# The work between two cross-attention layers moves pair by pair into the second attention's loop

## Chip, cores and metric

One core of one Trainium2 chip runs the program. The metric is device time in microseconds from launch to end; the median of three runs of the kernel before is given with the profile. TensorE (PE) multiplies matrices, VectorE (DVE), ScalarE (ACT) and GpSimd (POOL) do the elementwise work, and SyncE (SP) issues the DMAs. PE writes only to the eight PSUM banks, and POOL can't read them.

## The reference

Two layers over a batch of 16, with 56 queries of 128 numbers each and a context of 1500 rows of 96. Cut to what is computed:

```python
# layer 0 (16 heads of 8)
q, k, v = jnp.split(x @ w_qkv + b_qkv, 3, axis=-1)
x = layer_norm(x + mha(q, k, v) @ w_so + b_so, ln_g, ln_b)
ca = mha(x @ w_q + b_q, y @ w_k + b_k, y @ w_v + b_v) @ w_co + b_co   # y: context
x = layer_norm(x + ca, ln_g, ln_b)
h = relu(x @ w1 + b1)              # 128 -> 512
h = relu(h @ w2 + b2)              # 512 -> 512
x = layer_norm(x + h @ w3 + b3, ln_g, ln_b)
# layer 1 (16 heads of 64)
h = layer_norm(x, gamma, beta)
Q, K, V = h @ Wq, y @ Wk, y @ Wv   # split in heads
attn = softmax(Q K^T) / 8
x = x + (attn V) @ Wo + bo
```

## The kernel before

All 16 batches' queries are handled as 896 tokens, or as eight tiles of two batches (a pair, 112 tokens). The program is a row of blocks; at the end of each, all engines meet, and within one each engine works down its own queue in the order written, with semaphores between them.

1. Opening block and self-attention (to 69 us).
2. Block A (69 to 95 us, lines 687 to 747): projection, norm, and the first cross-attention's queries. PE makes the queries once as 128 rows (`a_all`, L704) and then once more for each of four groups of heads, three times replicated to 96 rows (`wq3`, L713). ACT writes the fp16 part of each (L744), DVE the rest below it (L727), into `Q16`. Between these stand three transposes of a context.
3. The first cross-attention's loop over batches (95 to 470 us). POOL lays the queries of the next batch out by head (`Qst`, L773, and `Qmx`, L350).
4. The block between the layers (470 to 579 us, lines 1044 to 1192). For all eight tiles at once: output projection, norm (mean and variance on DVE, root on ACT, reciprocal on DVE), the three products of the feed-forward network in fp32 over 448 columns at a time (L1088, L1096, L1103), two more norms, and, since each head's key product can be taken into the queries (`Wqk` = Wq Wk^T per head), 32 fp32 products that give every batch's queries in context space (L1127). ACT writes their fp16 part (L1161), DVE the rest (L1189), to the tensor `QK` for all batches. Beside them the weights are turned (L1076) and multiplied (L1109, L1116). The last 12 of these 32 products have the score pieces of batch 0 between them.
5. The second cross-attention's loop (579 to 1104 us): one pass per batch, `body(i, par)` with batch b = 2i + par, of 14 steps c on each engine. In step c (under 12) PE makes the transposed scores of 125 keys in two halves, of three fp16 products each (L1283 to L1285, three PSUM banks), ACT takes their exponential (L1376), and POOL, or DVE in each third step, splits off the low part (`Pl`, L1266 and L1465). From step 2 on PE multiplies chunk c - 2 with the context (L1301 to L1303, 63 products a step).

Beside that the softmax maximum of the next batch is found: 21 score pieces of 500 keys (`score_piece1`, L1005), two or three a step from step 1, in two banks in turn. DVE reduces each (`reduce_piece1`, L1014), and PE waits for it as the first line says:

```python
wait_for(pe, n_red, n * 21 + max(k - 1, 0))   # piece k needs k - 1 reductions
...
if has_b and c < NC:
    scores_t(i, par, c, 0)
for k in pieces[:1]:
    score_piece1(pe, i, par, k)
if has_b and c < NC:
    scores_t(i, par, c, 1)
```

The first piece of a step thus stands between the two halves of the scores. At step 10 DVE takes the maximum over the pieces (`negate_maximum`, L1439 to L1447), at step 12 PE turns it (L1333) and DVE lays it beside the queries (`lay_maximum`, L1452), for which the next batch's scores wait (`n_mlaid`). At the start of a batch DVE first divides the batch before by its sums (`finish_batch`, L1405 and L1409), at steps 4 to 7 PE, ACT and DVE turn that output in the bank W1, and in even batches PE projects a pair at step 8 (L1322) and DVE adds residual and bias at step 9 (L1423, L1427). SP loads the halves of the next batch's context and queries (`load_halves`, L994 and L997) as soon as the slot is free.

## Time and profile before

| | us |
|---|---|
| median of three runs | 1106.84 (1106.81 to 1107.83) |
| the profiled execution, its own time | 1106.37 |
| its span, first to last instruction | 1104.60 |
| before the first cross-attention (0 to 95.4) | 95.4 |
| first cross-attention (95.4 to 470.15) | 374.75 |
| between the layers (470.15 to 578.80) | 108.65 |
| second cross-attention (578.80 to 1104.60) | 525.80 |

The profile is of one execution; its instruction times are compared with its own time. Busy time is the sum of an engine's instructions; PE's are pipelined, and their ends modelled. A group is named by line, engine, operation and out<-in tiles. "[idle before <-releaser]" behind an instruction is the engine's idle time and who ended it. PEclk is the granted share of 2.4 GHz.

### The profile page before, as it was taken

To read this page: it belongs to the slowest core of one execution; us is meant where nothing else is said; L and a number is where in the kernel's file an instruction comes from. 1 tells how busy PE (TensorE), PEld (TensorE's weight loads), DVE (VectorE), ACT (ScalarE), POOL (GpSimd) and SP (SyncE) were. 2 spreads that over 40 slices of the span, in tenths; PEclk is the share of its full clock that TensorE was granted. 3 is DMA by queue.
4 is the path that set the end of the run, shared out by engine and by line. 5 is a ranking of instruction groups with operands and counts; after the bars stand their busy time and mean duration, and the time that the engine had idled before them with its cause. 6 is when DMAs were issued, how large, how long until landed. Compare 5 with 4: busy or idle time off the path is not lost. (4 is left out here: it accounts for less than half of the span.)

```text
span 1104.6 us, 31648 instructions
## 1 busy us (share of the span) xinstructions
PE 1026.3 (93%) x12060; PEld 742.5 (67%) x12060; DVE 748.1 (68%) x1409; ACT 571.4 (52%) x1139; POOL 389.8 (35%) x273
## 2 busy tenths in 40 slices
PE   5977899999999999979688999999999999999997
PEld 2552577777777776646325777777777778777786
DVE  4657788887888778321794776777676767767752
ACT  2533577777777776631444544445444444544442
POOL 4821121111211123030105554545455454646542
PEclk9988899999999999989798999999999999999998
DMA  3501544444444443030002111111111111012100
GB/s 105 144 2 70 145 133 135 126 152 140 128 132 139 141 123 91 2 99 1 0 23 76 56 56 38 55 38 39 54 56 54 41 49 51 28 52 56 35 4 4
DMA packets 48461, 79.41 MB, mean 72 GB/s; under 512 B 8802, under 2 KB 35252, under 8 KB 48404
## 3 DMA queue, kind: packets, MB, share of 16 engines
q1 hardware_dynamic: 48404, 78.61, 23.8%
q8 instruction: 40, 0.66, 0.3%
q14 instruction: 17, 0.14, 0.0%
HBM read 51.13 MB, written 21.96 MB: 66 GB/s over the span
## 5 line engine op out<-in xcount | busy, mean ns | idle before, releaser
L1376 ACT ACTIVATE P<-PS 125x448 f32<-125x448 f32 x384 | 207.1, 544 | 270.3 <-PE PS L1285 268.4
L1266 POOL TENSOR_TENSOR Pl<-P 125x896 f16<-125x896 f32 x128 | 229.9, 1801 | 242.3 <-ACT P L1376 242.3
L1014 DVE TENSOR_REDUCE m<-PS 128x1 f32<-128x500 f32 x336 | 220.8, 675 | 120.1 <-PE PS L1005 118.3
L920 DVE TENSOR_REDUCE m_part<-PS 128x1 f32<-128x500 f32 x336 | 210.5, 673 | 54.8 <-PE PS L822 53.3
L1301 PE MATMUL PS<-cNh,P 125*128 125x97 f16 x1344 | 198.0, 208 | 0.1
L1303 PE MATMUL PS<-cNh,Pl 125*128 125x97 f16 x1344 | 197.4, 207 | 0.0
L1302 PE MATMUL PS<-cNl,P 125*128 125x96 f16 x1344 | 196.8, 206 | 0.0
L898 ACT ACTIVATE Pb<-PS 125x448 f32<-125x448 f32 x384 | 186.0, 547 | 19.5 <-PE PS L797 18.5
L1302 PEld LDWEIGHTS PS<-cNl,P 125*128 125x128 bf16 x1344 | 131.9, 98 | 25.5 <-issue 0.2
L1301 PEld LDWEIGHTS PS<-cNh,P 125*128 125x128 bf16 x1344 | 131.2, 98 | 15.8 <-issue 3.2
L1283 PE MATMUL PS<-Qh,cTh 110*125 110x448 f16 x384 | 139.0, 362 | 1.3 <-DVE Qh L1452 1.3
L822 PE MATMUL PS<-KH,Qmx 128*128 128x500 f16 x336 | 129.2, 387 | 8.5 <-DVE m_part L920 4.1
L1284 PE MATMUL PS<-Ql,cTh 96*125 96x448 f16 x384 | 136.8, 356 | 0.0
L773 POOL TENSOR_TENSOR Qst<-Q,tab 96x224 f16<-96x224 f32 (+1 forms) x64 | 33.7, 556 | 289.6 <-DVE Qst L960 281.2
L1285 PE MATMUL PS<-Qh,cTl 96*125 96x448 f16 x384 | 135.6, 353 | 0.0
L1303 PEld LDWEIGHTS PS<-cNh,Pl 125*128 125x128 f16 x1344 | 131.1, 98 | 0.0
L1005 PE MATMUL PS<-cTh,Qh 96*128 96x500 f16 x336 | 119.3, 377 | 6.6 <-DMA Qh<-QK 3.5
L797 PE MATMUL PS<-Qst,Kst 110*125 110x224 f16 x768 | 110.8, 263 | 4.9 <-DMA Kst<-k_halves 2.1
L797 PEld LDWEIGHTS PS<-Qst,Kst 110*125 110x125 f16 x768 | 87.8, 136 | 30.4 <-ACT Pb L898 7.7
L808 PE MATMUL PS<-Pb,Vst 125*32 125x112 f32 x3072 | 93.3, 262 | 0.0
L1465 DVE TENSOR_TENSOR Pl<-P 125x896 f16<-125x896 f32 x64 | 70.3, 1099 | 28.3 <-ACT P L1376 28.2
L808 PEld LDWEIGHTS PS<-Pb,Vst 125*32 125x32 f32 x3072 | 70.4, 109 | 19.6 <-issue 15.4
(170 smaller groups left out, 1530.0 us busy)
## 6 DMA issues: line engine op xcount, KB each, us to landing
Kst<-k_halves SPq DMA_DIRECT2D x144, 125.0 KB, 2.8
k_halves<-KH SPq DMA_DIRECT2D x16, 750.0 KB, 3.2
cx<-in_ctx SPq DMA_DIRECT2D x16, 562.5 KB
d_cx<-in_ctx SPq DMA_DIRECT2D x16, 562.5 KB
c_halves<-cHi SPq DMA_DIRECT2D x16, 281.2 KB, 2.6
c_halves<-cLo SPq DMA_DIRECT2D x16, 281.2 KB, 3.0
cTh<-c_halves SPq DMA_DIRECT2D x16, 281.2 KB, 3.0
cTl<-c_halves SPq DMA_DIRECT2D x16, 281.2 KB, 3.8
```

What stands on the lines that cost most here:

```text
L797: mm = pe.matmul(PS[0:KC, u % 3, (g % 2) * 224:(g % 2 + 1) * 224], Kst[:, par, g, c * KC:(c + 1) * KC], Qst[:, par, g, :], start=True, sto ...
L808: mm = pe.matmul(PS[32 * (p % 4):32 * (p % 4) + 32, OB, (p // 4) * TP:(p // 4 + 1) * TP], Vst[:, par, c, p, :], Pb[:, c % NPB, p * TP:(p + ...
L898: nc.scalar.activation(Pb[:, c % NPB, half * HALF:(half + 1) * HALF], PS[0:KC, u % 3, 0:HALF], ACT.Exp, scale=SCALE0).then_inc(exp_done, 1)
L920: nc.vector.tensor_reduce(m_part[:, t, part:part + 1], PS[:, 6 + k % 2, 0:SP], AX.X, ALU.max).then_inc(s_reduced, 1)
L1014: nc.vector.tensor_reduce(m21[:, t, part:part + 1], PS[:, S1[k % 2], 0:SP], AX.X, ALU.max).then_inc(n_red, 1)
L1266: nc.gpsimd.tensor_tensor(Pl[:, c % NP], P1[:, c % NP], high, ALU.subtract).then_inc(n_low_p, 1)
L1283: pe.matmul(o, cTh[:, par, at], Qh[:, par, cols], start=True, stop=False)
L1284: pe.matmul(o, cTh[0:DC, par, at], Ql[:, par, cols], start=False, stop=False)
L1301: pe.matmul(o, high, cNh[:, par, c, :], start=(c == 0 and t % 4 == 0), stop=False, skip_group_check=True)
L1302: pe.matmul(o[:, 0:DC], high, cNl[:, par, c, :], start=False, stop=False, skip_group_check=True)
L1303: mm = pe.matmul(o, Pl[:, c % NP, cols], cNh[:, par, c, :], start=False, stop=(c == NC - 1), skip_group_check=True)
L1376: nc.scalar.activation(P1[:, c % NP, half * HALF:(half + 1) * HALF], PS[0:KC, u % 3, 0:HALF], ACT.Exp).then_inc(n_exp, 1)
```

## The change

- **Block A.** The four replicated products are gone, with `wq3` and `bq3`. ACT writes the fp16 part of the 128-row queries (`Qall`), DVE its rest (`Qrest`), and SP copies both group by group with twelve DMAs into `Q16`. POOL waits for them before the first `Qst`.
- **First attention.** POOL splits w1, w2 and w3, times 64, into two fp16 halves in batch 0 (`split_weights`).
- **Between the layers.** Only pair 0 goes all the way there, and pair 1 up to the second hidden layer. All feed-forward and query products use three fp16 products (high x high, high x low, low x high) in place of one fp32. The root of the variance is taken on DVE, by a guess from the bits and three Newton steps (`spread_of`), in place of ACT's root. `QK` for all batches becomes `QKs` for one pair. The halves and queries of batches 0 and 1 are both loaded here.
- **Second attention.** An odd batch 2i + 1 does the first part for pair i + 2 (`pair_ahead`): projection, `norm_cross`, hidden layers, and at its last step `hidden_3`. The even batch 2i + 2 does the second part for that pair (`pair_behind`, there i + 1): `norm_twice`, `turn_pair`, and in steps 3, 5, 7 and 10 `absorb`, which makes four heads' queries for both batches. All use the bank W1 in turn with the output's turning and projection, hence the added waits.

The diff, cut. Left out are declarations, the small helpers `out_project`, `turn_pair` (one PE operation each), `keep_pair` and `keep_hidden` (two and four ACT operations of 112 columns), `residual`, `take_attention`, `move_residual` (two, one and one POOL operations on 112 x 128), `hidden_3` (12 products as in `hidden_2`) and `queries_high` (one ACT copy of 448 columns), the removed lines of the block between, and its new PE, ACT and POOL queues, which have the same calls in the order of DVE's.

```diff
+                sp.wait_ge(a_high, 1)
+                for block_row in range(2):
+                    for g in range(G):
+                        sp.dma_start(Q16[32 * block_row:32 * block_row + 32, g, :], Qall[32 * g:32 * g + 32, :]).then_inc(q_in, 16)
+                sp.wait_ge(a_low, 1)
+                for g in range(G):
+                    sp.dma_start(Q16[64:96, g, :], Qrest[32 * g:32 * g + 32, :]).then_inc(q_in, 16)
...
+                    for n, (weight, halves) in enumerate(((w1s, w1x), (w2s, w2x), (w3s, w3x))):
+                        nc.gpsimd.tensor_scalar(weight[:], weight[:], WS, None, ALU.mult).then_inc(w_scaled, 1)
+                        pool.wait_ge(w_scaled, n + 1)
+                        nc.gpsimd.tensor_copy(halves[:, 0], weight[:]).then_inc(w_high, 1)
+                        pool.wait_ge(w_high, n + 1)
+                        nc.gpsimd.tensor_tensor(halves[:, 1], weight[:], halves[:, 0], ALU.subtract).then_inc(w_split, 1)
+                    nc.gpsimd.tensor_tensor(rows[:, R_B3, :], rows[:, R_B3, :], rows[:, R_B, :], ALU.add).then_inc(rows_added, 1)
...
-        def load_halves(sp, i, par, half, queries_made=None):
+        def load_halves(sp, i, par, half, ahead=False):
             slot, n = (par + 1) % 2, i * 2 + par + 1
             keys, queries = ((cTh, Qh), (cTl, Ql))[half]
-            if half == 0:
+            if half == 0 and not ahead:
                 wait_for(sp, n_st, (n - 1) * 2 * NC)
             at = bass.ds(n, 1)
             sp.dma_start(keys[0:DC, slot:slot + 1, :], c_halves[at, half].rearrange("b p k -> p b k")).then_inc(n_in[half][slot], 16)
-            if queries_made is not None:
-                sp.wait_ge(queries_made, H)
-            sp.dma_start(queries[0:DC, slot].rearrange("p (h q) -> p h q", h=H).unsqueeze(1), QK[:, half, at]).then_inc(n_in[half][slot], 16)
+            sp.wait_ge((g_high, g_low)[half], (i + (par + 1) // 2) * 4 + 4)
+            sp.dma_start(queries[0:DC, slot], QKs[:, half, slot].rearrange("p h q -> p (h q)")).then_inc(n_in[half][slot], 16)
...
+        def spread_of(dve, link, at, k, src):
+            dve.wait_ge(link, at)
+            nc.vector.bn_stats(st6[:, k], src).then_inc(link, 1)
+            dve.wait_ge(link, at + 1)
+            nc.vector.memset(passed[:], 0.0)
+            nc.vector.bn_aggr(mv[:, k], st6[:, k]).then_inc(link, 1)
+            dve.wait_ge(link, at + 2)
+            nc.vector.tensor_scalar(half_var[:, k:k + 1], mv[:, k, 1:2], EPS, -0.5, ALU.add, ALU.mult).then_inc(link, 1)
+            dve.wait_ge(link, at + 3)
+            nc.vector.tensor_scalar(root[:, k:k + 1].bitcast(I32), half_var[:, k:k + 1].bitcast(I32), -0.5, ROOT_GUESS, ALU.mult, ALU.add).then_inc(link, 1)
+            for n in range(ROOT_STEPS):
+                dve.wait_ge(link, at + 4 + 2 * n)
+                nc.vector.tensor_scalar(grown[:, k:k + 1], root[:, k:k + 1], root[:, k:k + 1], half_var[:, k:k + 1], ALU.mult, ALU.mult).then_inc(link, 1)
+                dve.wait_ge(link, at + 5 + 2 * n)
+                nc.vector.tensor_scalar(root[:, k:k + 1], grown[:, k:k + 1], 1.5, root[:, k:k + 1], ALU.add, ALU.mult).then_inc(link, 1)
+            dve.wait_ge(link, at + SPREAD)
+        def norm_cross(dve, t, bank):
+            dve.wait_ge(f_proj, t + 1)
+            nc.vector.tensor_tensor(wk[:].unsqueeze(1), PS[0:TP, bank, 0:D].unsqueeze(1), X[:, bass.ds(t, 1), :], ALU.add).then_inc(f_link, 1)
+            spread_of(dve, f_link, t * LINKS_A + 1, 0, wk[:])
+            nc.vector.tensor_scalar(nm[:], wk[:], mv[:, 0, 0:1], root[:, 0:1], ALU.subtract, ALU.mult).then_inc(f_normed, 1)
+        def split_pair(dve, t, k):
+            dve.wait_ge((f_kept, e_kept)[k], t + 1)
+            nc.vector.tensor_tensor(T16[:, k, 1], T32[:, k], T16[:, k, 0], ALU.subtract).then_inc((f_split, e_split)[k], 1)
+        def hidden_1(pe, t, bank):
+            pe.wait_ge(f_split, t + 1)
+            for m in range(4):
+                for n, (w, v) in enumerate(TERMS):
+                    mm = pe.matmul(PS[:, bank, m * TP:(m + 1) * TP], w1x[:, w, m * 128:(m + 1) * 128], T16[:, 0, v], start=(n == 0), stop=(n == 2))
+            mm.then_inc(f1, 1)
+        def hidden_2(pe, t, m, bank):
+            if m == 0:
+                pe.wait_ge(f1_split, t + 1)
+            for k in range(4):
+                for n, (w, v) in enumerate(TERMS):
+                    mm = pe.matmul(PS[:, bank, m * TP:(m + 1) * TP], w2x[:, w, k, m * 128:(m + 1) * 128], hid16[:, 0, v, k],
+                                   start=(k == 0 and n == 0), stop=(k == 3 and n == 2))
+            if m == 3:
+                mm.then_inc(f2, 1)
+        def split_hidden(pool, t, k):
+            kept, high, split = ((f1_kept, f1_high, f1_split), (f2_kept, f2_high, f2_split))[k]
+            pool.wait_ge(kept, t + 1)
+            nc.gpsimd.tensor_tensor(hid16[:, k, 0].rearrange("p m c -> p (m c)"), hid[:, k].rearrange("p m c -> p (m c)"),
+                                    one[:].broadcast_to([128, 4 * TP]), ALU.mult).then_inc(high, 1)
+            pool.wait_ge(high, t + 1)
+            nc.gpsimd.tensor_tensor(hid16[:, k, 1], hid[:, k], hid16[:, k, 0], ALU.subtract).then_inc(split, 1)
+        def norm_twice(dve, t, bank):
+            dve.wait_ge(f3, t + 1)
+            dve.wait_ge(f_residual, t * 2 + 2)
+            nc.vector.scalar_tensor_tensor(out=wk2[:], in0=PS[0:TP, bank, 0:D], scalar=1 / WS, in1=Xm[:], op0=ALU.mult, op1=ALU.add).then_inc(e_link, 1)
+            at = t * LINKS_B + 1
+            spread_of(dve, e_link, at, 1, wk2[:])
+            nc.vector.scalar_tensor_tensor(out=wk2[:], in0=wk2[:], scalar=mv[:, 1, 0:1], in1=rows[:, R_G, :],
+                                           op0=ALU.subtract, op1=ALU.mult).then_inc(e_link, 1)
+            dve.wait_ge(e_link, at + SPREAD + 1)
+            wait_for(dve, x_moved, t)
+            nc.vector.scalar_tensor_tensor(out=Xn[:], in0=wk2[:], scalar=root[:, 1:2], in1=rows[:, R_B, :],
+                                           op0=ALU.mult, op1=ALU.add).then_inc(e_link, 1)
+            spread_of(dve, e_link, at + SPREAD + 2, 1, Xn[:])
+            nc.vector.tensor_scalar(nm2[:], Xn[:], mv[:, 1, 0:1], root[:, 1:2], ALU.subtract, ALU.mult).then_inc(e_normed, 1)
+        def absorb(pe, t, r, bank):
+            if r == 0:
+                pe.wait_ge(e_split, t + 1)
+            for k in range(4):
+                for n, (w, v) in enumerate(TERMS):
+                    mm = pe.matmul(PS[0:DC, bank, k * TP:(k + 1) * TP], Wqk[:, w, 4 * r + k, :], T16[:, 1, v], start=(n == 0), stop=(n == 2))
+            mm.then_inc(g_made, 1)
+        def queries_low(dve, t, r, bank):
+            dve.wait_ge(g_high, t * 4 + r + 1)
+            if r == 0:
+                wait_for(dve, n_in[1][1], t * 32)
+            for j in range(2):
+                low = nc.vector.scalar_tensor_tensor(out=QKs[:, 1, j, 4 * r:4 * r + 4, :],
+                                                     in0=PS[0:DC, bank, 0:4 * TP].rearrange("p (h j q) -> p j h q", h=4, j=2)[:, j],
+                                                     scalar=1 / WS, in1=QKs[:, 0, j, 4 * r:4 * r + 4, :], op0=ALU.mult, op1=ALU.subtract)
+            low.then_inc(g_low, 1)
...
+                norm_cross(dve, 0, 0)
+                split_pair(dve, 0, 0)
...
+                norm_twice(dve, 0, 1)
+                norm_cross(dve, 1, W1)
+                split_pair(dve, 0, 1)
+                for r in range(4):
+                    queries_low(dve, 0, r, 1 - r % 2)
+                split_pair(dve, 1, 0)
+                for k in range(NPC):
+                    reduce_piece1(dve, -1, 1, k)
+        weights.close()
...
+                        has_p, t = pair_behind(i, par)
+                        if has_p and c == 2:
+                            move_residual(pool, t)
+                        has_p, t = pair_ahead(i, par)
+                        if has_p and c == 2:
+                            residual(pool, t)
+                            if not isinstance(t, int) or t + 1 < NT:
+                                take_attention(pool, t + 1)
+                        if has_p and c == 5:
+                            split_hidden(pool, t, 0)
+                        if has_p and c == 11:
+                            split_hidden(pool, t, 1)
+                over_pairs(pool, body, before=((-1, 1),), last=3)
...
+                        has_p, t = pair_behind(i, par)
+                        if has_p and c == 2:
+                            turn_pair(pe, t, 1, W1)
+                        if has_p and c in R_STEP:
+                            if has_old and c in (5, 7):
+                                pe.wait_ge(n_ot, (b - 1) * 2 + (c - 3) // 2)
+                            if has_old and c == 10:
+                                pe.wait_ge(n_y, i)
+                            elif not has_old and c > 3:
+                                pe.wait_ge(g_low, t * 4 + R_STEP[c])
+                            absorb(pe, t, R_STEP[c], W1)
+                        if has_p and has_old and c in (4, 6, 8):
+                            pe.wait_ge(g_low, t * 4 + c // 2 - 1)
+                        if has_b and has_old and c == 4 and pair_ahead(i, par)[0]:
+                            pe.wait_ge(f1_kept, pair_ahead(i, par)[1] + 1)
                         if has_b and has_old and c in (4, 6):
                             turn_output(b - 1, (c - 4) // 2)
                         if has_b and has_old and par == 0 and c == 8:
                             project(i - 1)
+                        if has_p and c == NC:
+                            pe.wait_ge(g_low, t * 4 + 4)
+                        has_p, t = pair_ahead(i, par)
+                        if has_p:
+                            if c == 0:
+                                out_project(pe, t, W1)
+                            if c == 2:
+                                turn_pair(pe, t, 0, W1)
+                            if c == 3:
+                                hidden_1(pe, t, W1)
+                            if c == 7:
+                                pe.wait_ge(n_ot, (b - 1) * 2 + 2)
+                            if 7 <= c < 11:
+                                hidden_2(pe, t, c - 7, W1)
+                            if c == NC:
+                                pe.wait_ge(f2_kept, t + 1)
+                        if isinstance(i, int) and b == -1 and c == NC:
+                            pe.wait_ge(f2_kept, 2)
                         if has_1 and c == NC:
                             turn_maximum(i, par)
+                        if c == NC + 1 and par == 1 and (has_p or (isinstance(i, int) and i < 0)):
+                            pe.wait_ge(n_mlaid, b + 2)
+                            hidden_3(pe, t, W1)
...
+                        has_p, t = pair_behind(i, par)
+                        if has_p and c == 0:
+                            norm_twice(dve, t, W1)
+                        if has_p and c == 3:
+                            split_pair(dve, t, 1)
+                        if has_p and c - 1 in R_STEP:
+                            queries_low(dve, t, R_STEP[c - 1], W1)
+                        has_p, t = pair_ahead(i, par)
+                        if has_p and c == 1:
+                            norm_cross(dve, t, W1)
+                        if has_p and c == 3:
+                            split_pair(dve, t, 0)
```

## Rows read from the trace of the kernel before

**Rows 1.** Busy time by engine; granted clock in 40 slices of the span.

```profile
PE 1026.3 (93%) x12060; PEld 742.5 (67%) x12060; DVE 748.1 (68%) x1409; ACT 571.4 (52%) x1139; POOL 389.8 (35%) x273
...
PEclk9988899999999999989798999999999999999998
```

**Rows 2.** Busy time by stretch: from:to, length, engines (instructions), clock, DMA share, GB/s.

```profile
470.15:578.80 108.65, 86.74 (x349) 46.08 (x349) 55.22 (x145) 36.08 (x55) 12.66 (x6) 0.91 0.11 31
...
742.30:806.10 63.80, 63.69 (x757) 49.65 (x756) 45.37 (x81) 29.81 (x58) 33.34 (x19) 1.00 0.15 48
...
588.00:592.60 4.60, 4.55 (x12) 2.50 (x13) 2.04 (x3) 1.09 (x2) 1.68 (x1) 0.50 0.02 8
```

**Rows 3.** Groups of the stretch between the layers: busy us, mean ns, idle before.

```profile
L1127 PE MATMUL PS<-T,Wqk 128*96 128x448 f32 x64 | 28.4, 581 | 0.2 <-DVE T L667 0.2
```

**Rows 4.** Order of time from 470 us: start us, us, instruction.

```profile
477.17 0.88 PE L1076 MATMUL PS<-tab,Wvs 96*128 96x96 f32 x8 [0.57 <-DMA Wvs<-in_L_xattn_Wv]
...
481.08 2.25 PE L623 MATMUL PS<-tab,normed 112*128 112x112 f32 x8 [3.03 <-DVE normed L657]
...
555.41 0.66 SPq L997 DMA_DIRECT2D Qh<-QK  x1
...
558.41 0.59 PE L1005 MATMUL PS<-cTh,Qh 96*128 96x500 f16 x2
...
588.04 0.60 PE L1005 MATMUL PS<-cTh,Qh 96*128 96x500 f16 x1 [3.45 <-DMA Qh<-QK]
```

**Rows 5.** Order of time in block A, and the first of the next.

```profile
84.36 1.01 ACT L741 ACTIVATE Qall<-PS,bq 128x896 f16<-128x896 f32 x1 [3.46 <-PE PS L704]
...
95.44 0.30 SPq L231 DMA_DIRECT2D cx<-in_ctx  x1
```

**Rows 6.** Order of time around a batch boundary of the second attention, at 746.20.

```profile
744.05 0.38 PE L1333 MATMUL PS<-tab,mn 128*14 128x128 f32 x2
744.36 0.22 PE L1301 MATMUL PS<-cNh,P 125*128 125x97 f16 x1
...
744.84 1.10 DVE L1452 TENSOR_TENSOR Qh<-PS,tab 14x896 f16<-14x896 f32 x1
...
746.20 0.38 PE L1283 MATMUL PS<-Qh,cTh 110*125 110x448 f16 x1
...
746.68 0.92 DVE L1409 SCALAR_TENSOR_TENSOR On<-PS,r 128x384 f32<-128x384 f32 x2
...
748.19 3.32 POOL L1266 TENSOR_TENSOR Pl<-P 125x896 f16<-125x896 f32 x2 [4.89 <-ACT P L1376]
748.44 2.15 DVE L1014 TENSOR_REDUCE m<-PS 128x1 f32<-128x500 f32 x3 [0.84 <-PE PS L1005]
...
749.50 0.37 PE L1005 MATMUL PS<-cTh,Qh 96*128 96x500 f16 x1
```

**Rows 7.** DVE operations by line: min/median/max ns; then groups, busy and mean ns.

```profile
L1441 DVE TENSOR_SCALAR mt<-mt x16: 170/171/1691, 579.4 to 1060.5; 128x7 f32<-128x7 f32 x16
...
L629 DVE BATCH_NORM_STATS2 sums<-work 112x6 f32<-112x128 f32 x16 | 3.5, 281 | 0.1
...
L1174 DVE SCALAR_TENSOR_TENSOR work<-work,mean_var,rows 112x128 f32<-112x128 f32 x8 | 2.2, 348 | 0.0
```

**Rows 8.** DVE and POOL in order of time at one `negate_maximum`.

```profile
677.61 0.17 DVE L1439 TENSOR_REDUCE mt<-m 128x7 f32<-128x21 f32 x1
677.80 1.68 POOL L1266 TENSOR_TENSOR Pl<-P 125x896 f16<-125x896 f32 x1 [0.48 <-ACT P L1376]
677.81 1.69 DVE L1441 TENSOR_SCALAR mt<-mt 128x7 f32<-128x7 f32 x1
```

**Rows 9.** PE in order of time in the projection of a pair.

```profile
669.31 0.27 PE L1322 MATMUL PS<-Wvo,OTh 96*112 96x128 f16 x2
669.42 0.22 PE L1322 MATMUL PS<-Wvo,OTl 96*112 96x128 f16 x1
669.48 0.28 PE L1322 MATMUL PS<-Wvo,OTh 96*112 96x128 f16 x2
```

357 lines of the change are left out of this document (195 added, 162 removed).

## The prediction

> **What bounds the kernel now.** I read the busy table and the clock line first, then the busy time by stretch, then the order of instructions where one stretch ends and around one batch boundary of the second attention. The reader is to see three things. TensorE is the busiest engine and the clock line falls below full speed in a few places only [rows 1]. The work between the layers is one stretch, 470.15 to 578.80 us: 108.65 us, in which the vector engine (DVE) works for 55.2 us and the scalar engine (ACT) for 36.1 us, so it is loosely packed; its fp32 products are the largest groups, such as the 64 records of L1127 with 28.4 us [rows 2, 3]. The second attention is the opposite: in a pair of batches of 63.8 us TensorE is busy for 63.69 us at clock 1.00, DVE for 45.37, ACT for 29.81, GpSimd (POOL) for 33.34 [rows 2]. So whatever TensorE does more in that loop is paid in full, and so is every wait put in its queue; what leaves the stretch between is gained in full.
>
> **The sum's base.** The profiled execution took 1106.37 us (span 1104.60, so 1.8 around it); the median of the runs is 1106.84. About 0.2%, some 2 us, is what a measurement of this kernel can tell from no change.
>
> **1. Queries of the first layer.** From the start of the Qall activation at 84.36 to the next block at 95.44 are 11.1 us [rows 5], with four projections of 96 rows, four ACT and four DVE steps taking turns. After the change one ACT and one DVE step of that size remain (done by 86.7), then three transposes of the context with their copies (about 89), while SP, freed at 85.4, issues twelve DMAs. At the 0.4 us that neighbouring issues stand apart (the one of Qh took 0.66) [rows 4] that is 90.3, and the block ends near 90.8. Gain 4.6 us; bounds 2.5 (0.6 us an issue) and 6.5 (the copies end last). That POOL then waits for these DMAs costs nothing: its Qst is needed only once the maxima are laid some 20 us later. The splitting of the FFN weights on POOL stands early in batch 0 of the first attention and takes 10 to 18 us by POOL's 1.68 us for 896 columns [rows 8]; the next Qst is wanted two batches on, so 0, with 4 us as the upper end.
>
> **2. The stretch between the layers.** Only pair 0 and half of pair 1 stay. Step by step: weights landed, turned and copied as before until 478.9 (the last turning is in [rows 4]), pair 0 turned and split at 479.8; first hidden layer, its activations and POOL's two splitting steps beside the head products, 484.1; 48 products of the second layer 3.6, activations 1.0, splitting 1.8, third layer 1.1: 491.6; `norm_twice` 6.2 (below), 497.8; `norm_cross` of pair 1, which the DVE queue has ahead of `split_pair`, 3.1, and that split: 501.2; four rounds of `absorb`, copy and difference, 5.3: 506.5; from the issue of the Qh load to the first score piece 3.0, as now (555.41 to 558.41) [rows 4]: 509.5; 21 reductions of 0.68, 14.2, with a hole of about 3 where pair 1's `hidden_2` stands between pieces 8 and 9: 526.8. In this chain a set of four activations is put at 1.0 (a 112-column copy takes 0.25), a splitting by POOL at twice 0.9 (half of 1.68) [rows 8], products at 50 to 100 ns. So 56.7 in place of 108.65, gain 52.0. Bounds 44 and 58: this is one serial chain, and much of its TensorE work will be at half clock.
>
> **3. First batch of the second attention.** TensorE waits 3.45 us for the Qh load of batch 1 [rows 4]. Now that load is issued in the block before. Gain 3.4.
>
> Gains together: 60.0 us.
>
> **4. More TensorE work in the loop.** Per pair `absorb` has 48 fp16 products, the hidden layers 12 + 48 with 112 moving columns and `hidden_3` 12 with 128. The projection's 128-column products start 56 ns apart at full clock (three in 0.17 us) [rows 9], so I take 50 ns for 112 columns. The half behind (`turn_pair`, `absorb`) is 2.5 us, the half ahead (`out_project`, `turn_pair`, `hidden_1`, `hidden_2`, `hidden_3`) 4.0. Seven pairs have the first in the loop, six the second, and pair 1's `hidden_3` comes ahead of it: 17.5 + 24.0 + 0.7 = 42.2 us. Nothing hides it; the other ends are 36 and 50.
>
> **5. The wait for `norm_twice`.** It stands in the DVE queue at step 0 of each even batch, behind `finish_batch` and ahead of all reductions of that batch. TensorE reaches score piece 2 at 749.50, 3.30 us after the boundary at 746.20 [rows 6]; that piece waits until the reduction of piece 0 is over. DVE ends `finish_batch` 1.40 after the boundary (746.68 + 0.92 less 746.20) [rows 6]. Then come 26 dependent instructions: 20 small ones of 0.17, a sum and two statistics of 0.28, three of 0.35 [rows 7], each 0.03 to 0.04 after the one it waits for (677.61 + 0.17 to 677.81) [rows 8]: 3.4 + 0.84 + 1.04 + 0.9 = 6.2. With one reduction of 0.68 [rows 6] piece 2 may start at 1.40 + 6.2 + 0.68 = 8.3, that is 5.0 us late. Behind the waiting piece stand the scores of step 2 and everything after it; ACT and POOL starve with it.
>
> The upper end comes from POOL. L1441, the same operation, takes 171 ns at the median and 1691 at most [rows 7]: at 677.81 it ended with POOL's instruction that had started at 677.80 [rows 8]. In the loop POOL runs two such from 748.19 for 3.32 us [rows 6], just when the chain is in its scalar steps: the first two would be held until 5.4 after the boundary in place of 2.7, stall 7.6. Whether a step on one element per partition is held too no row shows (L1441 has seven); the wide steps late in the chain are. I take the middle, 6.3. Seven of them, less 1.2 in batch 0, which has no `finish_batch` ahead: 42.9 us. The Trainium skill (SBUF — State Buffer, Who interferes with whom) has the pair of ports that DVE and GpSimd share as an exclusive lock for copies, casts and `tensor_scalar` in two-port modes and for two SBUF inputs; L1441's 1691 ns agrees. By that rule with every step held, this term would be 52.0.
>
> **6. The wait for `norm_cross`.** The same place in the odd batches, 13 instructions: 1.7 + 0.56 + 0.35 + 0.45 = 3.1. Piece 2 starts at 1.40 + 3.1 + 0.68, against 3.30 plus 0.22 of `out_project`: 1.6 late, 4.2 with POOL's two instructions. Middle 2.9, six times: 17.4 us.
>
> The Trainium skill (VectorE: DVE Perf Modes, The TRN2 errata) gives an SBUF step 58 cycles plus its columns, some 61 ns for one element by its table. This trace has 171 ns for seven [rows 7], so the table isn't used. By it the two chains would be 1.8 and 0.9 us shorter, and the time about 18 us below mine.
>
> **7. The clock after those waits.** After TensorE's idle 3.03 us before 481.08, and again from 588.00 to 592.60 after 3.45 us, matmuls ran at the lower level (granted 0.50, that is 1.2 of 2.4 GHz) [rows 2, 4]; the loop runs at 1.00 without a fall. Stalls of 3 to 7 us make it fall. Each low stretch lasts some 5 us beyond the stall, so 0 (DVE is behind then anyway) to 2.9 us lost; I take 1.6, thirteen times: 20.8 us.
>
> **8. `hidden_3` behind the maximum.** It waits for DVE's laying of the maximum, which ends at 744.84 + 1.10 = 745.94, while TensorE has only 21 products from 744.36, 0.93 us, to do first [rows 6]: 0.7 late, six times: 4.2 us. Today 21 more hide it. The other handovers of the shared bank (`absorb`, `turn_output`, `project`) have a step of 2.6 us between them and DVE work of at most 2.3: 0, at most 1 us a pair. DVE itself would have about 35 us of work in an even batch, as much as TensorE, so such small waits are the likeliest thing I miss.
>
> **Sum.** 1106.4 - 60.0 + 42.2 + 42.9 + 17.4 + 20.8 + 4.2 = 1173.9 us, 6% slower.
>
> **Rivals.**
> - *Short waits* (18%): no one-element step is held by POOL and the clock hardly falls: 33.8 + 9.6 + 6.5 for terms 5 to 7, 1142.7 us. For it: the small forms are nowhere seen held. Against it: idle stretches as short as 3.03 us were followed by the low level.
> - *Long waits* (17%): all steps held, 2.9 us of clock each time, and the stretch between at its worse end with 7 us less gained: 52.0 + 25.2 + 37.7, 1214.7 us. Against it: POOL has only two instructions to give in that window before it starves.
> - *Faster* (7%): DVE's chains stay out of TensorE's way, so terms 5, 6 and 7 vanish and 1106.4 - 60.0 + 42.2 + 4.2 = 1092.8. It decides at one point: the chain must be over 2.6 us after the boundary, so within 1.2 us behind `finish_batch`. For it speaks only that DVE is idle for 18 of 63.8 us; against it that the idle time lies elsewhere and 26 dependent steps of 0.2 can't fit.
> - *The stretch between hardly shrinks, or small gains meet* (3%): within 2 us of before. It would need a gain in 2 of opposite size to the waits.
>
> The forecast has 55%. The range of 8 in 10 is 1138 to 1206: it takes in the short waits and most of the way to the long ones. Faster 0.08 and same 0.03 follow from the last two rivals and a little for error in the method; slower 0.89.
>
> **What would show it.** Second attention: pair periods near 84 us in place of 63.8, with TensorE idle before the third score piece of each batch, released by DVE, longest in even batches; granted clock below 1 behind it; TensorE pitch of about 50 ns in the new products. Between: about 57 us. If that wait is under 1 us, terms 5 to 7 are wrong; if small steps in `spread_of` never exceed 0.2 us, POOL does not hold them; if the stretch is over 70 us, step 2 is.

## The result, and the profile after

| | before | after |
|---|---|---|
| median of the runs, us | 1107.34 (1106.81 to 1108.38, 4 runs) | 1173.15 (1171.12 to 1173.91, 4 runs) |
| profiled execution: span, mean granted clock | 1104.6, 0.969 | 1169.3, 0.934 |

The ratio is 1.059, its 95% interval 1.0572 to 1.0609: slower, at nearly the time forecast (1173.9). Four stretches carry the 64.7 us between the spans: up to the first attention's first load 0.7, the first attention 0.9, the work between the attentions -50.0, the second attention +113.1. For the last two the stretch between ends with VectorE's last reduction, at 530.37, as the 578.80 of the kernel before does.

Busy time and clock line of the changed kernel, which answer to [rows 1]: TensorE has only 13 us more busy time, but the clock line falls in places all along the second half.

```profile
PE 1039.4 (89%) x12796; PEld 777.3 (66%) x12796; DVE 802.0 (69%) x1676; ACT 582.1 (50%) x1216; POOL 450.4 (39%) x345
...
PEclk8976999999999999757998999999989989989998
```

Busy time by stretch, columns as in [rows 2]: the work between the layers, batch 9 and batch 10 of the second attention.

```profile
471.77:530.64 58.87, 36.73 (x296) 26.54 (x296) 29.74 (x86) 16.51 (x35) 16.35 (x20) 0.66 0.27 73
...
899.19:937.02 37.83, 34.85 (x431) 27.50 (x430) 25.25 (x53) 17.63 (x39) 23.04 (x16) 1.00 0.17 49
937.02:981.48 44.46, 38.40 (x455) 29.97 (x453) 32.74 (x76) 17.81 (x35) 16.97 (x10) 0.92 0.10 29
```

The stretch between is 58.87 us where it was 108.65 [rows 2]; this window ends at the next block's first DMA issue, 0.3 us behind that reduction. In the loop an odd batch took 30.49 us before and takes 37.83, an even one took 33.33 and takes 44.46. TensorE was idle for at most 0.11 us in such a batch; now it is idle for 2.98 and 6.06 us. No branch back stands before either of these; over the pairs from batch 2 to batch 11 the time runs from 76.7 to 87.7 us, as the low clock and the branch fall. Which instructions it is idle before, the groups of TensorE from 534.8 us on say (busy, mean ns, idle before and releaser):

```profile
L1454 PE MATMUL PS<-Qh,cTh 110*125 110x448 f16 x384 | 144.3, 376 | 10.0 <-issue 10.0
L1027 PE MATMUL PS<-cTh,Qh 96*128 96x500 f16 x315 | 115.6, 390 | 35.9 <-DVE m L1036 35.8
...
L1145 PE MATMUL PS<-w3x,hid 128*112 128x128 f16 x74 | 5.7, 225 | 3.8 <-DVE Qh L1671 3.8
```

L1027 is the score piece: 35.9 us of waiting for VectorE's reductions, 5.99 in batches 2, 10 and 12, 3.76 in batch 0 and 2.34 in each odd batch to 11. L1145 is `hidden_3` behind the maximum, six times 0.63. L1454 is a batch's first score product: 10.0 us with no releaser at all, before batches 4, 6 and 8. Order of time of the even batch 10, DVE and TensorE mixed, answering to [rows 6]:

```profile
938.34 0.28 DVE L1168 SCALAR_TENSOR_TENSOR wk<-PS,Xm 112x128 f32<-112x128 f32 x1
...
939.00 3.32 POOL L1425 TENSOR_TENSOR Pl<-P 125x896 f16<-125x896 f32 x2 [3.90 <-ACT P L1583]
...
939.40 0.15 DVE L1075 TENSOR_SCALAR root<-half_var 112x1 int32<-112x1 int32 x1
939.59 0.27 DVE L1078 TENSOR_SCALAR grown<-root,half_var 112x1 f32<-112x1 f32 x1
939.89 0.21 DVE L1080 TENSOR_SCALAR root<-grown,root 112x1 f32<-112x1 f32 x1
...
941.26 1.20 DVE L1171 SCALAR_TENSOR_TENSOR wk<-wk,mv,rows 112x128 f32<-112x128 f32 x1
942.50 0.35 DVE L1175 SCALAR_TENSOR_TENSOR Xn<-wk,root,rows 112x128 f32<-112x128 f32 x1
...
945.48 0.34 DVE L1178 TENSOR_SCALAR nm<-Xn,mv,root 112x128 f32<-112x128 f32 x1
945.74 2.04 DVE L1036 TENSOR_REDUCE m<-PS 128x1 f32<-128x500 f32 x3
...
946.47 0.60 PE L1027 MATMUL PS<-cTh,Qh 96*128 96x500 f16 x1 [6.00 <-DVE m L1036]
946.86 0.58 PE L1454 MATMUL PS<-Qh,cTh 110*125 110x448 f16 x1
```

The reader sees the chain of 26 instructions from 938.34 to 945.8 (24 in turn, and two `memset` steps of 0.06 us that run beside others), the reduction behind it, and TensorE let go at 946.47. The one-element steps keep their 0.15 to 0.27 us while POOL works; L1171, with two SBUF operands, ends at 942.5, just behind POOL's end at 942.3. The score products then take 0.58 us for 0.35: the clock has fallen. Over the whole program, min/median/max in ns:

```profile
L1078 DVE TENSOR_SCALAR grown<-root,half_var x72: 272/272/274, 476.0 to 1028.8; 112x1 f32<-112x1 f32 x72
L1080 DVE TENSOR_SCALAR root<-grown,root x72: 214/214/215, 476.3 to 1029.1; 112x1 f32<-112x1 f32 x72
L1171 DVE SCALAR_TENSOR_TENSOR wk<-wk,mv,rows x8: 352/776/1759, 498.0 to 1025.2; 112x128 f32<-112x128 f32 x8
```

No one-element step was ever held; the 128-column step with two SBUF operands was, by up to 1.4 us.

### The profile page after: what moved, and what is told of

It is laid out like the page before. It is cut to its first block, busy times and chain, and to the rows that moved or that the text cites. A ratio compares the mean times of both kernels' runs of the same rounds, so it can differ in the third digit from the quotient of the medians.

```text
span 1169.3 us, 33324 instructions
## 1 busy us (share of the span) xinstructions
PE 1039.4 (89%) x12796; PEld 777.3 (66%) x12796; DVE 802.0 (69%) x1676; ACT 582.1 (50%) x1216; POOL 450.4 (39%) x345
## 3 DMA queue, kind: packets, MB, share of 16 engines
q8 instruction: 81, 1.33, 0.5%
## 4 chain that ended last, share of the span: by engine, by line
PE 44%; DVE 7%; issue 3%; ACT 0%; DVEq 0%; POOL 0%; ACTq 0%
PE PS L1454 6%; PE PS L1027 6%; PE PS L1455 6%; PE PS L1456 5%; PE PS L1472 5%; PE PS L1474 5%; PE PS L1473 5%; PE PS L1493 2%; PE PS L1192 2%; DVE m L1036 1%; PE PS L1136 1%; DVE grown L1078 1%; PE PS L1485 1%; DVE root L1080 1%; DVE Qh L1671 1%
## 5 line engine op out<-in xcount | busy, mean ns | idle before, releaser
L1425 POOL TENSOR_TENSOR Pl<-P 125x896 f16<-125x896 f32 x128 | 226.8, 1775 | 301.8 <-ACT P L1583 301.7
L1472 PE MATMUL PS<-cNh,P 125*128 125x97 f16 x1344 | 202.7, 210 | 0.1
L1474 PE MATMUL PS<-cNh,Pl 125*128 125x97 f16 x1344 | 202.0, 209 | 0.0
L1473 PE MATMUL PS<-cNl,P 125*128 125x96 f16 x1344 | 201.4, 208 | 0.0
L903 ACT ACTIVATE Pb<-PS 125x448 f32<-125x448 f32 x384 | 186.1, 548 | 20.1 <-PE PS L802 18.6
L1027 PE MATMUL PS<-cTh,Qh 96*128 96x500 f16 x336 | 125.6, 397 | 39.2 <-DVE m L1036 38.9
L1454 PE MATMUL PS<-Qh,cTh 110*125 110x448 f16 x384 | 144.3, 376 | 10.0 <-issue 10.0
L1455 PE MATMUL PS<-Ql,cTh 96*125 96x448 f16 x384 | 141.3, 368 | 0.0
L1456 PE MATMUL PS<-Qh,cTl 96*125 96x448 f16 x384 | 139.5, 363 | 0.0
```

Of the source, the lines that this page charges most:

```text
L1027: pe.matmul(PS[:, S1[k % 2], 0:SP], Qh[0:DC, slot, t * 128:(t + 1) * 128], cTh[0:DC, slot, part * SP:(part + 1) * SP], start=True, stop=Tr ...
L1425: nc.gpsimd.tensor_tensor(Pl[:, c % NP], P1[:, c % NP], high, ALU.subtract).then_inc(n_low_p, 1)
L1454: pe.matmul(o, cTh[:, par, at], Qh[:, par, cols], start=True, stop=False)
L1455: pe.matmul(o, cTh[0:DC, par, at], Ql[:, par, cols], start=False, stop=False)
L1456: pe.matmul(o, cTl[:, par, at], Qh[0:DC, par, cols], start=False, stop=True).then_inc(n_st, 1)
L1472: pe.matmul(o, high, cNh[:, par, c, :], start=(c == 0 and t % 4 == 0), stop=False, skip_group_check=True)
```

## The experiments

All times are medians; a ratio is to the kernel before on the same chip, with its 95% interval.

**1. The chain shorter.** `ROOT_STEPS` 3 to 0; the Newton steps are left out of the computation.

```
-        ROOT_STEPS = 3
+        ROOT_STEPS = 0
```

> Leaves out the three Newton steps of every reciprocal root (six one-element instructions a spread: 12 of norm_twice's 26, 6 of norm_cross's 13), all else as in the changed kernel (1173.15 us). Theory (the third score piece waits for VectorE's chain, and the chain's length is what the stall costs): at 0.15 to 0.27 us each, about 1.4 us a spread go. The stalls of 5.99 us in batches 2, 10 and 12 fall to 3.4 to 4.3, that of batch 0 from 3.76 to about 1, the six of 2.34 to 0.9 to 1.4; batches 4, 6 and 8, where TensorE stands still over 3 us at the loop's back edge anyway, gain at most 1; the work between the attentions loses 3 to 5. Together 18 to 25 us with some clock returned: 1148 to 1155. Rival A (GpSimd's hold of a two-input instruction, not the chain's length, sets when the chain ends): the stalls stay within 0.5 us, only the stretch between gains, 1168 to 1170. Rival B (the low clock is what costs, and any shorter idle ends it): the stretches at half clock vanish from the loop, 1135 or less.

Measured 1137.26 us (ratio 1.0267, 1.0237 to 1.0298), 36 us less than the changed kernel. Its score-piece group, and around batch 2:

```profile
602.73 1.24 DVE L1171 SCALAR_TENSOR_TENSOR wk<-wk,mv,rows 112x128 f32<-112x128 f32 x1
604.00 1.65 DVE L1175 SCALAR_TENSOR_TENSOR Xn<-wk,root,rows 112x128 f32<-112x128 f32 x1
...
607.60 0.60 PE L1027 MATMUL PS<-cTh,Qh 96*128 96x500 f16 x1 [3.98 <-DVE m L1036]
...
L1027 PE MATMUL PS<-cTh,Qh 96*128 96x500 f16 x315 | 113.4, 383 | 16.2 <-DVE m L1036 16.2
```

Waits fell by 19.7 us (35.9 to 16.2), the stretch between by 4.7. The stalls went the theory's way, 5.99 to 3.98 and 2.34 to 0.70 (a little below its 0.9 to 1.4), and that of batch 0 is gone. Six steps are worth 1.64 us; twelve gave only 2.0 in `norm_twice`, because the two steps with two SBUF operands came earlier into POOL's work and were held longer, 1.24 and 1.65 us. The time lies 11 us below the theory's range and near rival B, but the low clock did not vanish: its time in batches 0 to 12 fell from 58.1 to 34.8 us, and TensorE's busy time there from 481.2 to 471.7 with the same products. That 9.4 us is what the shorter waits gave back in clock, more than I had allowed.

**2. POOL's hold taken away.** The chain's sum goes to PSUM, so that L1171 reads one SBUF operand.

```
+            w = PS[0:TP, bank, D:2 * D]
...
-            nc.vector.scalar_tensor_tensor(out=wk2[:], in0=wk2[:], scalar=mv[:, 1, 0:1], in1=rows[:, R_G, :],
+            nc.vector.scalar_tensor_tensor(out=w, in0=w, scalar=mv[:, 1, 0:1], in1=rows[:, R_G, :],
...
```

> The changed kernel with one edit: the sum that norm_twice norms lies in a free part of the shared PSUM bank and no longer in SBUF, so no instruction of the chain but the last reads two operands from SBUF (the last has one tensor and two scalars per partition). Same instructions, same order. Theory (VectorE's step with two SBUF operands is held until GpSimd's instruction ends, the one-element steps are not): L1171's record of 1.20 us in batches 2, 10 and 12 falls to about 0.35, the stall there from 5.99 to 5.1 to 5.2, and the time by 3 to 5 us with some clock: 1168 to 1171. Rival (the whole chain is slowed evenly by GpSimd, whatever its operands): no record changes, 1172 to 1174.

Measured 1168.59 us (ratio 1.0542, 1.0525 to 1.0558). In batch 2 the step takes 0.36 us and the stall is 5.15 (5.99):

```profile
614.86 0.21 DVE L1080 TENSOR_SCALAR root<-grown,root 112x1 f32<-112x1 f32 x1
615.11 0.36 DVE L1172 SCALAR_TENSOR_TENSOR PS<-PS,mv,rows 112x128 f32<-112x128 f32 x1
615.50 0.35 DVE L1176 SCALAR_TENSOR_TENSOR Xn<-PS,root,rows 112x128 f32<-112x128 f32 x1
```

In all eight pairs it takes 0.36 us (357 to 360 ns), where it had reached 1.76. So this step is held for its second SBUF operand, and that is worth 0.84 us a chain, not the 2.6 of the forecast's upper end. The 4.6 us between the medians is not resolved into its parts: the profiled spans differ by 1.2 us only (1168.1 and 1169.3), and in this execution batch 6 waits 2.56 us for VectorE behind its branch, which it did not in the changed kernel's.

**3. No branch back.** Pairs 1 to 4 are written out for the four compute engines.

```
-    with eng.Fori(1, NT - last) as i:
-        body(i, 0)
-        body(i, 1)
-    for i in range(NT - last, NT):
+    for i in range(1 if last == 3 else NT - last, NT):
         body(i, 0)
         body(i, 1)
```

> The second attention's loop over pairs 1 to 4 is written out on TensorE, ScalarE, VectorE and GpSimd, with no branch back; nothing else changes. Theory (the 3.2 to 3.5 us in which TensorE waits for nothing ahead of batches 4, 6 and 8 come from the branch back and the fetch of instructions behind it): these three gaps vanish, and the wait before the third score piece, which they hid, shows in their place with 5.99 us each: 8 us slower, 1177 to 1183. Rival (the gap is something else, a missing record or a wait): batches 4, 6 and 8 keep it, 1172 to 1175. Second rival (written-out code has to be fetched all through and costs elsewhere): above 1190, with gaps without releaser spread over the loop.

Measured 1179.09 us (ratio 1.064, 1.0612 to 1.0668). The groups:

```profile
L1455 PE MATMUL PS<-Qh,cTh 110*125 110x448 f16 x384 | 144.1, 375 | 0.0
L1028 PE MATMUL PS<-cTh,Qh 96*128 96x500 f16 x315 | 116.4, 393 | 53.5 <-DVE m L1037 53.5
```

The 10.0 us are gone and the stall of 5.99 stands in batches 4, 6 and 8 too (35.9 + 3 x 5.9 = 53.6). The branch stall was real, and in the changed kernel it lies over part of the chain's.

**4. One product for three** (two of three are left out of the computation).

```
-        TERMS = ((0, 0), (0, 1), (1, 0))
+        TERMS = ((0, 0),)
```

> Leaves out two of the three fp16 products of hidden_1, hidden_2, hidden_3 and absorb (80 of 120 products a pair), all else as in the changed kernel. Theory (TensorE is full from batch to batch but for the stalls, so each product costs its 49 ns pitch): 3.9 us a pair over 6.5 pairs, 25 us, and 2 to 5 us between the attentions; stalls as they were: 1142 to 1147. If the 3.3 us at the loop's back edge are the fetch of a longer instruction stream, they shrink as well, but the wait for norm_twice that they cover then shows, so the time changes by no more than 6 us for it. Rival (the products fill time in which TensorE would wait for the exponentials or for VectorE anyway): 1160 or more.

Measured 1144.62 us (ratio 1.0338, 1.0294 to 1.0382), in the theory's range. Its parts fit less well: 6.5 us went between the end of the first attention and batch 0 (2 to 5 forecast) and 18.4 in batches 0 to 12 (25), and of the 28.1 us between the profiled spans 3.2 lie ahead of that, where the code is the same. Batch 9 of this kernel:

```profile
881.57:917.16 35.59, 32.40 (x385) 25.00 (x383) 25.29 (x53) 17.34 (x39) 22.86 (x16) 1.00 0.16 49
```

TensorE's busy time there is 2.45 us less than the 34.85 above for 48 products less: 51 ns each. TensorE is full but for the stalls, and every product is paid: over batches 0 to 12 its busy time is 21.6 us less although it is at the lower clock a little longer (63.9 us, not 58.1). The stalls at the branch did not shrink with the shorter body: 3.71 to 3.87 us, against 3.23 to 3.51.

**5. fp32 hidden layers.** One fp32 product for three fp16 ones.

```
-                for n, (w, v) in enumerate(TERMS):
-                    mm = pe.matmul(..., w2x[:, w, k, ...], hid16[:, 0, v, k], ...)
+                mm = pe.matmul(..., w2s[:, k, ...], hid[:, 0, k], ...)
```

> The three hidden layers of the pair are computed with one fp32 product each in place of three fp16 ones: 24 products a pair instead of 72; splitting steps stay, the queries stay in three fp16 products. Theory (an fp32 product of 112 columns costs what two fp16 ones cost, by the 112 ns mean of out_project's record in the changed kernel): 24 times 0.11 is 2.7 us in place of 3.5, so 0.9 us less a pair over six pairs: 1165 to 1170. Rival (an fp32 product costs four passes of 49 ns each): 4.7 in place of 3.5, 1.2 us more a pair, and as much in the stretch between: 1179 to 1185.

Measured 1192.02 us (ratio 1.0763, 1.0747 to 1.0778), 19 us more than the changed kernel: the rival's direction, and 7 us beyond its range; the theory is out. Batch 9, and the group of `hidden_3`:

```profile
915.69:955.94 40.25, 36.62 (x408) 29.63 (x406) 25.89 (x53) 17.65 (x39) 22.14 (x16) 1.00 0.18 50
...
L1145 PE MATMUL PS<-w3s,hid 128*112 128x128 f32 x49 | 7.2, 287 | 7.7 <-DVE Qh L1671 7.7
```

1.77 us more of busy time in each odd half, 10.6 over six; the wait before `hidden_3` doubled (3.9 more), that of batch 0 grew by 1.6, the time between the first attention and batch 0 by 3.1. With 60 products at 49 ns and 12 at 56, an fp32 product of this size cost (3.6 + 1.8) / 24 = 0.22 us, against 0.15 for three fp16 ones. The record's mean of 112 ns, on which my theory stood, isn't its price. So in this place the three fp16 products are the cheaper form, and it isn't they that make the change a loss.

**6. The same work in another order.** VectorE reduces the first two pieces in the middle of each chain (`between`), and the pair's transpose goes to the end of key tile 2 (`weave`):

```
-            spread_of(dve, e_link, at, 1, wk2[:])
+            spread_of(dve, e_link, at, 1, wk2[:])
+            between()
...
+                        if c == 2 and pair_behind(i, par)[0]:
+                            turn_pair(pe, pair_behind(i, par)[1], 1, W1)
```

> VectorE reduces the first two score pieces of a batch in the middle of norm_twice or norm_cross instead of behind it, and TensorE's transpose of the normed pair moves from the middle of the third key tile to its end. The work is the same. Theory (the stalls are a matter of order on VectorE: nothing but the third piece needs the reduction, and nothing needs the chain's end before the transpose): the stalls before the third piece fall from 5.99 to under 2 us and from 2.34 to under 1, a part comes back at the transpose, and the clock stays up more: 20 to 35 us less, 1138 to 1153. Rival (the transpose becomes the place of the same wait, because the chain of 7.5 us outlasts three key tiles): 1165 to 1172, the wait now ahead of the transpose. If all of it went, 1115.

Measured 1154.49 us (ratio 1.0413, 1.0387 to 1.044). The next version writes the pairs out and moves score pieces and the shared bank's users of even batches later (`shift_unrolled`):

```
+        LATE1 = [range(NPC * min(max(c - 3, 0), 8) // 8, NPC * min(max(c - 2, 0), 8) // 8) for c in range(NC + LAG)]
...
+                        c1 = c - (1 - par)
-                        if has_p and c == 2:
+                        if has_p and c1 == 2:
                             turn_pair(pe, t, 1, W1)
```

> The same work in another order, and pairs 1 to 4 written out. In even batches the 21 score pieces stand beside key tiles 3 to 10 in place of 1 to 9, and all that uses the shared bank (transpose of the pair, the four absorb groups, the old heads' transposes, the projection) comes one key tile later; in odd batches VectorE reduces the first two pieces in the middle of norm_cross, and the pair's transpose comes at the end of key tile 2. Theory (all stalls are places where TensorE's queue has a piece or a transpose ahead of the end of a VectorE chain, and the gaps at the back edge are the branch): the waits of 5.99, 3.76 and 2.34 us (35.8 in all) and the three gaps (10) go, and the clock behind them stays up (20 of the 24 us that it cost): 1105 to 1120. Rival A (the three pieces in one key tile wait for each other, 1 to 2 us an even batch, because each needs the reduction of the last but one): 1120 to 1130. Rival B (the clock falls all the same, from short waits): 1130 to 1140. Not below 1105: 42 us of added products stand against 50 from the stretch between.

Measured 1146.06 us (ratio 1.034, 1.0321 to 1.0359). The last one adds experiment 2 and puts both transposes at the end of their key tile (`shift2`):

> As the version with the shifted even batches and written-out pairs (1146.06 us), with the transpose of the normed pair at the end of its key tile in both halves (key tile 3 in even, 2 in odd batches) and norm_twice's sum in PSUM. Theory (what was left of the stalls stood ahead of the transposes: 2.70 us in each even batch, 1.50 in each odd, and 0.90 ahead of the first absorb group): under 1 us remains of each, the low clock of batches 0, 2, 6 and 10 goes: 1118 to 1128. Rival (the wait only moves on to the first absorb group and to hidden_1, which need the transposed pair 2 to 3 us later): 1135 to 1145. Either way above the kernel before, since about 45 us of added products remain.

Measured 1144.2 us (ratio 1.0328, 1.0312 to 1.0344). Each time the wait before the score piece went (in `weave` down to 4.8 us) and another came: the groups of the three kernels with more than 4 us of idle time before them, beside `hidden_3`.

```profile
L1456 PE MATMUL PS<-Qh,cTh 110*125 110x448 f16 x384 | 141.8, 369 | 9.9 <-issue 9.9
L1027 PE MATMUL PS<-cTh,Qh 96*128 96x500 f16 x315 | 113.5, 384 | 4.8 <-DVE m L1036 4.8
L1110 PE MATMUL PS<-tab,nm 112*128 112x112 f32 x13 | 4.2, 323 | 21.0 <-DVE nm L1180 18.5 <-DVE nm L1099 2.5
```

```profile
L1111 PE MATMUL PS<-tab,nm 112*128 112x112 f32 x13 | 4.4, 336 | 27.4 <-DVE nm L1180 18.3 <-DVE nm L1100 9.0
```

```profile
L1111 PE MATMUL PS<-tab,nm 112*128 112x112 f32 x13 | 4.1, 313 | 6.8 <-DVE nm L1181 4.4 <-DVE nm L1100 2.3
L1195 PE MATMUL PS<-T,Wqk 128*96 128x112 f16 x336 | 24.2, 229 | 17.9 <-DVE T L1122 17.9
```

In the last, `split_pair` stands on VectorE behind a `Pl` step that the chain had pushed back, and that takes 2.44 us there beside POOL's own `Pl` from 610.96, where its median is 1.08; `split_pair` itself takes 1.15 us for 0.27. Both read two SBUF operands:

```profile
611.15 2.44 DVE L1704 TENSOR_TENSOR Pl<-P 125x896 f16<-125x896 f32 x1
...
615.31 0.98 PE L1195 MATMUL PS<-T,Wqk 128*96 128x112 f16 x8 [2.94 <-DVE T L1122]
```

`weave` came 1.5 us above its theory's range, `shift_unrolled` 26 above and beyond both rivals, `shift2` into its rival's range: I counted the wait that I moved, not what came late behind it. Whether a full rearrangement of VectorE's queue would bring it under the kernel before was not tried.

**7. The parts that stand alone.** The kernel before with the first part of the change only (the projection of the queries, with twelve DMAs):

```
+                for block_row in range(2):
+                    for g in range(G):
+                        sp.dma_start(Q16[32 * block_row:32 * block_row + 32, g, :], Qall[32 * g:32 * g + 32, :]).then_inc(q_in, 16)
```

> The kernel before with only the first part of the change: one projection of all query rows, whose two halves twelve DMAs of SyncE put in their places. Theory (each issue takes SyncE 0.63 us, so the block lasts as long as before within 2 us; what it gains is lost at the start of the next): the same within 0.2% of the kernel before, 1105 to 1108.5. Rival (the forecast's step 1): 4.6 us less, 1102 to 1104.

Measured 1107.95 us (ratio 0.9995, 0.9985 to 1.0005): no change. In its execution the time from the Qall activation to the next block is 9.3 us, 1.8 less than before, and the stretch between the layers 1.4 longer, with 3.4 us more of low clock. SP's issues in it, and the first product of the next block:

```profile
85.42 5.06 SPq L688 DMA_DIRECT2D Q<-Qall  x8
...
90.53 2.49 SPq L691 DMA_DIRECT2D Q<-Qrest  x4
...
93.86 0.99 PE L810 MATMUL PS<-KH,Qmx 128*128 128x500 f16 x2 [8.23 <-PEq L682]
```

The kernel before with the load of batch 1's halves in the block between:

```
                 load_halves(sp, -1, 1, 1, g_low)
+                for half in range(2):
+                    load_halves(sp, 0, 0, half)
```

> The kernel before with one edit: the halves of keys and queries of batch 1 are loaded in the block between the attentions and not at the start of the second. Theory (that load is all that TensorE's 3.45 us wait at 588.04 is for, and the half clock before it has the other cause of the stretch before): 3.4 us less, 1103 to 1104.5. Rival (the two extra loads delay those of batch 0, or the maxima of the batch before are late instead): within 1 us of before.

Measured 1103.16 us (ratio 0.9953, 0.994 to 0.9966), 5.2 less. Batch 0 of the second attention, in the kernel before and, second, in this one:

```profile
581.73:618.48 36.75, 33.30 (x347) 23.84 (x348) 19.56 (x31) 14.11 (x25) 17.75 (x10) 0.86 0.21 63
```

```profile
583.35:614.90 31.55, 31.55 (x347) 23.29 (x348) 19.54 (x31) 14.11 (x25) 17.77 (x10) 0.95 0.15 49
```

It is 5.20 shorter: the wait of 3.45, and 1.75 of TensorE's busy time because the clock is 0.95 and no longer 0.86. (The span of this execution is only 3.6 us shorter: its first 97 us, where the code is the same, took 1.5 longer.) Both, with `Qrest` issued by ScalarE:

```
-                    sp.dma_start(Q16[64:96, g, :], Qrest[32 * g:32 * g + 32, :]).then_inc(q_in, 16)
+                    act.dma_start(Q16[64:96, g, :], Qrest[32 * g:32 * g + 32, :]).then_inc(q_in, 16)
```

> The kernel before with the load of batch 1's halves in the block between (alone 1103.16 us) and the first part of the change with its twelve DMAs issued by two engines, eight by SyncE and four by ScalarE. Theory (SyncE's 0.63 us an issue set the block's end, so four issues on another queue give 2.5 us, and 1.9 us that the block gained in the first trial are kept): 1099 to 1101.5. Rival (the block's gain is given back in the clock, as with the first part alone): 1102.5 to 1104.

Measured 1100.22 us (ratio 0.9935, 0.9921 to 0.9948), clearly below the kernel before. Against the early load alone (0.9940 to 0.9966) the intervals overlap, so that the second queue adds something is likely and not shown. The two queues run side by side:

```profile
87.21 5.29 SPq L688 DMA_DIRECT2D Q<-Qall  x8
88.40 2.53 ACTq L733 DMA_DIRECT2D Q<-Qrest  x4
...
93.34 0.99 PE L810 MATMUL PS<-KH,Qmx 128*128 128x500 f16 x2 [5.60 <-PEq L682]
```

## Why the prediction was right

The mechanism is shown: VectorE's dependent chain makes TensorE wait before the third score piece, the clock falls behind such waits, TensorE's new products are paid in full, and the stretch between gives 50 us back. That the total came within 1 us is luck. Against the spans, steps 1 (with the 0.9 us of the first attention), 2 and 4 (with 1.6 us around the loop) came out 6.2, 2.0 and 4.8 us dearer than forecast, steps 5, 6, 7 and 8 11.2, 3.4, 0.7 and 0.4 us cheaper: 13 us one way and 16 the other.

- **Step 1 (queries of the first layer), forecast -4.6:** wrong. The changed kernel has `Q<-Qall` from 87.92 for 5.05 us and `Q<-Qrest` from 93.02 for 2.49: 0.63 us an issue, not 0.4, so SP ends at 95.5. From the Qall activation to the next block it still is 1.8 us shorter (9.27 for 11.08), but the part alone is 0 within 1 us (experiment 7). The mis-sized term is the issue. The 0.4 is the pitch of the weight loads issued from 470 us on (0.40 to 0.48), of another form; [rows 4], named for it, shows only the 0.66. Its own bound had 0.6.
- **Step 2 (between), forecast -52.0:** measured -50.0. `norm_twice` alone took 6.65 (forecast 6.2), without any hold.
- **Step 3 (load of batch 1), forecast -3.4:** the wait is gone; alone it gave 5.2 with the clock, which the sum had left out.
- **Step 4 (TensorE's work), forecast +42.2:** measured 6 x 4.36 (odd batch, 34.85 against 30.49 busy) + 7 x 2.75 = 45.4, and 1.5 more ahead of batch 0, where pair 1's `hidden_3` stands. The even batch is read where nothing disturbs it, batch 4 of experiment 1, against 33.33:

```profile
681.87:717.95 36.08, 36.01 (x452) 28.60 (x452) 26.49 (x53) 17.66 (x35) 16.91 (x10) 1.00 0.11 33
```

- **Step 5 (wait for `norm_twice`), forecast +42.9:** 21.7 before the score piece and 10.0 at the branch back, 31.7. The chain was longer (7.5 us with 0.85 of hold, against 6.2 without: the Newton steps take 0.27 and 0.21 us, not 0.17), and the stall with it 6.0, near the 6.3 taken. That nearness is luck too: 6.3 was the middle between no hold (5.0) and two instructions of POOL (7.6), and neither was the case. The two sentences that go by the Trainium skill's table have one element at 61 ns; one-element steps took 150 to 270 ns, and with the prediction's own 0.17 the difference would be 2.2 and 1.1 us a chain, not 1.8 and 0.9. What was missed is three batches of seven: behind the branch TensorE stood still 3.2 to 3.5 us while VectorE, which did not wait, worked off the chain. In batch 8:

```profile
857.11 0.25 DVE L1624 RECIPROCAL r<-PS 128x4 f32<-128x4 f32 x2 [1.89 <-PE PS L1474]
...
860.36 0.63 PE L1454 MATMUL PS<-Qh,cTh 110*125 110x448 f16 x1 [3.29 <-issue]
```

- **Step 6 (`norm_cross`), forecast +17.4:** 6 x 2.34 = 14.0. The 2.9 was again a middle; the chain took 3.7 us (forecast 3.1), of which its last step is 0.76 beside POOL for 0.35, and it began 1.7 us after the boundary, not 1.4.
- **Step 7 (clock), forecast +20.8:** 20.1. Batches 0 to 12 in the kernel before and, second, in the changed one:

```profile
581.73:1001.49 419.76, 415.64 (x4884) 321.67 (x4884) 291.98 (x511) 193.10 (x373) 217.91 (x118) 0.99 0.17 50
534.79:1066.09 531.30, 481.16 (x5679) 374.07 (x5678) 375.24 (x840) 228.98 (x475) 255.77 (x165) 0.95 0.13 39
```

TensorE's busy time is 65.5 us more, of which 45.4 is work, so 20.1 is left. The clock agrees: it is granted 0.50 for 58.1 us of these batches, against 10.2 before, and TensorE works in 47.1 and 6.8 us of them; half of the difference is 20.1. The count behind the forecast was wrong, though: thirteen falls of 1.6 us. Of the six waits of 2.34 us three (batches 1, 5 and 9) were followed by no fall, batch 0 has as much low clock as before (10.4 us), and behind other waits the low stretch lasts 3.4 to 10.2 us. One of its two rows was also read wrongly: in the kernel before the clock was at 0.50 from 582.5 on, ahead of the 3.45 us wait, which began at 584.6:

```profile
582.50:584.50 2.00, 2.00 (x6) 0.92 (x4) 0.00 (x0) 1.09 (x2) 0.51 (x2) 0.50 0.93 244
```
- **Step 8 (`hidden_3`), forecast +4.2:** 3.8.

Of the rivals, *short waits* had its first condition right (no one-element step is held) and failed at the clock, which did fall; *long waits* failed at POOL's hold: [rows 8] showed a seven-element step held, and no one-element step was. The Trainium skill (SBUF — State Buffer, Who interferes with whom) says that a DVE instruction with two SBUF inputs contends with a GpSimd one that reads SBUF, and one with at most one input outside the two-port modes does not. Experiment 2 agrees: 1.20 against 0.36 us for the same step. *Faster* needed the chain out of TensorE's way, and three orders (experiment 6) didn't find one. Pair periods near 84 us, a sign that the prediction named, came for batches 10 and 11 alone (83.9); the four pairs before took 76.7 to 87.7.

## What to carry to other kernels

Work that fills no gap of the bound engine costs all of its time in a packed loop, and its dependent chain of small vector steps costs again as a wait of what is queued behind it, and a third time in the clock; loose serial work outside the loop can be the cheaper place. Before moving work, look for the wait that the move happens to remove: here one early load gave 5 us by itself. A stall taken out of one place has to be followed through the queue of the engine that caused it, since three times it came back further down the same queues (experiment 6).
